# A fused macaron block on one core: GpSimd's long pieces cut in two, the second norm's deviation moved, and the work laid out again

## The chip, the cores and the metric

The kernel runs on one core of one Trainium2 chip. The metric is the device time of one execution in microseconds (us), from the median of several runs. Engines are named as in the profile: PE is TensorE's matmul side, PEld its weight loads, DVE is VectorE, ACT is ScalarE, POOL is GpSimd, SP is SyncE, which only issues DMAs here.

## What is computed

The input is `x` with 2048 tokens of 256 numbers, float32. Three residual steps follow one another:

```python
x = x + 0.5 * ffn(layernorm(x), W_gate, W_qkv)
x = x + attn(layernorm(x), gamma, beta, W_in, b_in, W_out, b_out, W_skip, b_skip)
x = x + 0.5 * ffn(layernorm(x), W_gate, W_qkv)
```

`ffn` is in truth a causal attention with 16 heads of width 16. A softmax over 16 gates picks for every token one head's key and value (the value times the gate), which all 16 query heads share:

```python
idx = argmax(softmax(x @ W_gate.T))
q, k, v = split(x @ W_qkv.T)
k_shared, v_shared = k[idx], gate[idx] * v[idx]
att = softmax(where(causal, q @ k_shared / 4, -inf))      # for each of 16 heads
y = att @ v_shared
```

`attn`, called the branch here, is a gated recurrence: it normalizes its input a second time (so the deviation of the first norm is needed too), computes three gates of width 128 through `W_in`, scans `h = (1 - a) * h + a * b` over the tokens, multiplies with a tanh, projects through `W_out` and adds `x @ W_skip` and two biases.

## The kernel before, in words

**Tiles.** The tokens form four chunks `c` of 512 (4 tiles of 128). `l` is 0 or 1 for the two attention layers and 2 for the branch. `x_sb` holds the whole of x on the chip and is updated in place. An attention unit is (layer, chunk, group of 4 heads), 32 in all; a step is one unit and one tile of 128 keys, 320 steps in all, the first four of each unit on the causal diagonal.

**The work items.** Everything is cut into items, and one list, `ORDER`, says in which order they are issued. Each engine's program is a loop over `ORDER` that takes the items it has a part in, so an engine runs them strictly one behind the other. The items that matter here:

- `("qk", s, k)`: scores of step `s` for a pair of heads, PE line 1670; ACT takes the exponential into `probs` (line 1160, 1024 numbers per partition for a full tile); in a diagonal step POOL then zeroes what lies above the diagonal (the mask, `affine_select`, line 929).
- `("pv", s)`: PE multiplies `probs` with the values (line 1682). It waits for the exponential and, in a diagonal step, for the mask (`s_msk`). `probs` has four buffers.
- `("max", u, n)`: scores with queries on the rows, PE line 1648, so that DVE can take each query's maximum before the exponentials of that unit (`TENSOR_REDUCE`, line 1370, or an add of the mask with a maximum, line 1373); one kind goes through ACT (`relu`, line 1148).
- `("oev", u)`, `("fin", u)`: a unit's sums leave PSUM, are transposed and divided, and POOL adds them to `x_sb` (line 935).
- `prepare(l, c)`: norm, gates, choice of the head, queries and keys of a chunk. `stats` is DVE's mean and variance and then POOL's power to -0.5 (lines 891 and 892), `norm` is ACT's scaling into `u` (line 1042). `halve` is POOL's work for six of the eight chunks: it writes `u` as two float16 parts, a cast and a subtraction over 1024 numbers per partition (lines 941 and 942); `turn` (two, one for each half of the 256 features) are PE's transposes that wait for it. `choose` is DVE's sum over heads (line 1340).
- `branch(c)`: `stats` and `norm` as above, `turn`, `gates` (PE line 1614, then tanh on ACT, then `keep` and `alpha` on POOL, lines 995 and 996, then DVE), `scan` (DVE, then a multiplication on POOL, line 1001), `skip` and `rec` (two each, PE into PSUM; ACT moves `skip` into `sk`, DVE adds `rec` to `x_sb`), `add` (POOL adds `sk` to `x_sb`, 1024 numbers, line 1006).
- `("bias",)`: once, POOL prepares the branch's biases and scales `w_in_sb` (lines 976 to 980).
- `("warm", ...)`: matmuls into banks that nobody reads (lines 1487 and 1490), put where the planner expects PE to be idle.

**Two things POOL does for the branch in the kernel before.** Right behind `stats` of the branch it computes the deviation `s1` for the second norm (lines 895 to 897, needed only by `skip`), and at `norm` it adds the summed biases to the chunk's `x_sb` (line 988, 1024 numbers, needed only by `rec`).

**What sets the order.** `weave()` lays `ORDER` out before the kernel is built. It keeps a clock for each engine and for the PSUM banks, looks a few items ahead and picks what leaves the engines idle least (`LOSS` weighs them); `WEIGHT` says how long each item keeps each engine, `needs` what it depends on, `SIDE_WORK` from which step on the preparations and branches may begin. In the kernel before the masks are no work for POOL in that table: a diagonal `pv` is only held to 850 ns behind its scores instead of 240 (`TO_PE`); `add` and `halve` are entered with POOL times, the deviation, the branch's `norm` and `bias` are not.

## Time and profile before

| what | value |
|---|---|
| median of 3 runs | 934.8 us (933.85 to 934.95) |
| the profiled execution's own time | 931.48 us |
| its span in the trace | 929.6 us |
| mean granted TensorE clock | 0.96 of full |
| PE busy | 860.4 us, 93% of the span |
| DVE busy | 798.4 us, 86% |
| ACT busy | 709.0 us, 76% |
| POOL busy | 212.8 us, 23% |

The profiled execution took 1.9 us more than its span. Two engines are near full, so busy shares alone do not tell what a microsecond on a third one is worth; for that one looks at stretches in which both PE and DVE are idle, and at who ends the idle time. The granted clock is either full or half in any stretch.

### The profile page before, as it was taken

The numbers are of one execution on the slowest core, as the hardware profiler recorded it, in microseconds if no ns is written. First come the engines' busy times: TensorE is split into PE (matmuls) and PEld (weight loads), VectorE is DVE, ScalarE is ACT, GpSimd is POOL, SyncE is SP. The second block draws the span as 40 slices with busy tenths as digits, with TensorE's granted clock in tenths as the row PEclk, the third lists the DMA queues.
The fourth block names the chain that finished last, engine by engine and source line by source line (L and its number), as shares of the span: only waits on it lengthen the run. The fifth ranks groups of instructions, "written<-read, shape, count | busy, mean of one in ns | idle before, by whom it ended". The sixth has DMA issues, their size and how long they took to land.

```text
span 929.6 us, 18195 instructions
## 1 busy us (share of the span) xinstructions
PE 860.4 (93%) x6212; PEld 287.3 (31%) x6212; DVE 798.4 (86%) x2271; ACT 709.0 (76%) x1186; POOL 212.8 (23%) x422
## 2 busy tenths in 40 slices
PE   8897798989899989999999999989799999999997
PEld 6432223222233432223332243333332222222221
DVE  5998898999899789999867999979799999999920
ACT  2264376688879769997789867758689999999997
POOL 2032233111304322032212234144421101110110
PEclk9896689998999999999999999999899999999999
DMA  6110000100010001000010000100020000000000
GB/s 181 47 58 1 1 1 12 48 1 2 1 58 2 1 18 41 2 1 1 2 41 18 2 2 1 59 1 24 1 81 1 2 1 2 24 2 2 1 2 24
DMA packets 20235, 17.97 MB, mean 19 GB/s; under 512 B 4128, under 2 KB 20144, under 8 KB 20144
## 3 DMA queue, kind: packets, MB, share of 16 engines
q1 hardware_dynamic: 19328, 16.00, 5.7%
q8 instruction: 51, 0.84, 0.4%
q10 hardware_dynamic: 816, 0.80, 0.2%
q14 instruction: 40, 0.33, 0.1%
HBM read 10.24 MB, written 6.29 MB: 18 GB/s over the span
## 4 chain that ended last, share of the span: by engine, by line
PE 33%; DVE 13%; issue 7%; ACT 6%; POOL 2%; DMA 0%; POOLq 0%; SPq 0%; DVEq 0%; ACTq 0%
PE ps L1682 13%; PE ps L1648 8%; PE ps L1670 7%; DVE ps L1373 5%; ACT probs L1160 4%; DVE mxp L1370 3%; PE ps L1614 2%; DVE mxp L1373 1%; ACT relu L1148 1%; DVE kv L1340 1%; PE ps L1621 1%; PE ps L1657 1%; PE ps L1566 1%; PE ps L1628 1%; PE ps L1490 1%
## 5 line engine op out<-in xcount | busy, mean ns | idle before, releaser
L1160 ACT ACTIVATE probs<-ps 128x1024 f32<-128x1024 f32 (+5 forms) x841 | 553.9, 735 | 107.3 <-PE ps L1670 102.9
L1370 DVE TENSOR_REDUCE mxp<-ps 128x1 f32<-128x512 f32 x512 | 321.2, 684 | 35.6 <-PE ps L1648 31.3
L1682 PE MATMUL ps<-probs,v_l 128*32 128x512 f32 (+3 forms) x2560 | 306.3, 555 | 19.3 <-POOL probs L929 17.2
L1648 PE MATMUL ps<-k_tl,q_t 48*128 48x512 f16 (+3 forms) x1152 | 253.6, 358 | 12.7 <-DVE mxp L1373 4.6
L1670 PE MATMUL ps<-q_t,k_tl 50*128 50x512 f16 (+3 forms) x1280 | 245.0, 359 | 16.4 <-DMA q_t<-m_row 6.6
L1373 DVE CUSTOM_DVE_ANT_0 ps<-ps,mask 128x384 f32<-128x384 f32 (+3 forms) x512 | 233.6, 525 | 12.5 <-PE ps L1648 11.1
L929 POOL TENSOR_SCALAR_AFFINE_SELECT probs<-probs 128x256 f32<-128x256 f32 x256 | 102.2, 410 | 492.5 <-ACT probs L1160 490.2
L1648 PEld LDWEIGHTS ps<-k_tl,q_t 48*128 48x128 f16 x1152 | 74.1, 95 | 194.7 <-DVE mxp L1370 77.9
L1670 PEld LDWEIGHTS ps<-q_t,k_tl 50*128 50x128 f16 x1280 | 65.0, 94 | 190.5 <-ACT probs L1160 82.7
L1373 DVE DVE_READ_ACCUMULATOR2_ANT mxp<- 128x1 f32 x640 | 90.5, 141 | 0.0
L1373 DVE CUSTOM_DVE_ANT_0 ps<-ps,relu 128x512 f32<-128x512 f32 x128 | 85.8, 717 | 3.2 <-PE ps L1648 2.4
L1682 PEld LDWEIGHTS ps<-probs,v_l 128*32 128x32 f32 x2560 | 53.0, 109 | 107.8 <-issue 82.8
L1148 ACT ACTIVATE relu<-ps 128x512 f32<-128x512 f32 x128 | 71.6, 621 | 4.3 <-PE ps L1648 3.8
L1397 DVE RECIPROCAL rec<-ps 128x16 f32<-128x16 f32 x32 | 8.1, 252 | 39.1 <-PE ps L1657 38.8
L935 POOL TENSOR_TENSOR x_sb<-x_sb,y_att 128x256 f32<-128x256 f32 x32 | 23.3, 727 | 72.5 <-DVE y_att L1401 72.4
L1648 PE MATMUL ps<-kd_tl,q_t 48*128 48x512 f16 x128 | 37.7, 389 | 1.6 <-ACT probs L1160 0.9
L1566 PE MATMUL ps<-wqkv_x,ut_x 128*128 128x512 f16 x144 | 35.1, 380 | 0.5 <-DVE prod L1331 0.3
L1340 DVE TENSOR_REDUCE kv<-prod 128x32 f32<-128x512 f32 x32 | 32.6, 1019 | 0.7
L1168 ACT ACTIVATE o_sb<-ps 128x512 f32<-128x512 f32 x32 | 19.5, 609 | 11.7 <-PE ps L1682 11.7
L1042 ACT ACTIVATE u<-x_sb,shift,rstd 128x256 f32<-128x256 f32 x48 | 25.0, 609 | 2.9 <-POOL shift L892 2.9
L1657 PE MATMUL ps<-ident,o_sb 128*128 128x128 f32 x128 | 22.3, 301 | 2.1 <-DVE mxp L1373 0.7
L1331 DVE TENSOR_TENSOR prod<-ps,pick 128x512 f32<-128x512 f32 x32 | 21.9, 686 | 2.5 <-PE ps L1566 1.7
(167 smaller groups left out, 557.1 us busy)
## 6 DMA issues: line engine op xcount, KB each, us to landing
q_t<-q_scratch SPq DMA_DIRECT2D x96, 64.0 KB, 2.2
q_scratch<-q_part SPq DMA_DIRECT2D x16, 256.0 KB, 2.2
x_sb<-in_L_attn_x_dram SPq DMA_DIRECT2D x4, 512.0 KB, 8.3
out_dram<-x_sb SPq DMA_DIRECT2D x4, 512.0 KB, 3.0
q_t<-m_row SPq DMA_DIRECT2D x64, 4.0 KB
wqkv_n<-in_L_ffn_W_qkv_dram ACTq DMA_DIRECT2D x1, 768.0 KB, 6.9
w_in_sb<-in_L_attn_W_in_dram SPq DMA_DIRECT2D x1, 384.0 KB, 6.0
w_skip_sb<-in_L_attn_W_skip_dram SPq DMA_DIRECT2D x1, 256.0 KB, 5.5
```

Of the source, the lines that this page charges most:

```text
L929: g_.affine_select(out=pr, in_=pr, compare_op=ALU.is_ge, fill=0.0, base=0, pattern=[[0, 2], [1, P]], channel_multiplier=-1).then_inc(s_msk, 1)
L1042: last = a_.activation(u[:, t, :], x_sb[:, TC * c + t, :], ACT.Identity, scale=rstd[:, t:t + 1], bias=shift[:, t:t + 1])
L1148: a_.activation(relu[:, n % RELU_BUFS, :], bank_of(e), ACT.Relu).then_inc(s_ra, 1)
L1160: last = a_.activation(out if len(banks) == 1 else out[:, n:n + 1, :], bank[:, :, P * i:QW], ACT.Exp, scale=SCALE / LIFT ** 2)
L1340: last = v_.tensor_reduce(kv[:, t, :].rearrange("p (a d) -> p a d", a=2), prod[:, :].rearrange("p (a h d) -> p a d h", a=2, h=H), axis=AX, ...
L1370: last = v_.tensor_reduce(to, scores, axis=AX, op=ALU.max)
L1373: last = v_.tensor_tensor_reduce(scores, scores, added, 1.0, LOWEST, ALU.add, ALU.max, accum_out=to)
L1566: last = mm(bank[:, :], ut_x[:, dc, a, t * P:(t + 1) * P], wqkv_x[:, b, dc, D:3 * D], start=n == 0, stop=n == 3 * DC - 1)
L1648: last = mm(bank[:, col:col + w], q_rows(ROWS_X, c, g, hh, i * P, P), keys, start=True, stop=True)
L1657: last = tr(bank[:, i * P:(i + 1) * P], o_sb[:, i * P:(i + 1) * P], ident[:, :])
L1670: last = mm(ps[:, BANK[e][n], P * i:QW], k_cols(ROWS_XM, hh, l, kt, P), q_rows(ROWS_XM, c, g, hh, P * i, QW - P * i), start=True, stop=True)
L1682: last = mm(out_bank[VW * hh:VW * hh + VW, P * i:QW], v_l[:, l, kt, :], probs[:, s % NB, hh, P * i:QW], start=j == 0, stop=j == key_tiles( ...
```

## The change

- `halve` becomes two items, one for each half of the features. Each casts and subtracts 512 numbers per partition, and each `turn` waits only for its own half.
- The branch's `norm` loses its POOL part. It becomes two items `bsum`, 512 numbers each, behind the two `turn`; each `rec` waits for its own.
- The deviation leaves `stats` and becomes an item `dev` behind the first of the `gates`. From the second branch on it waits until ACT has read the former deviation.
- `add` becomes two items of 512 numbers, each behind its own `rec` and `skip`; `stats` of the next layer waits for both.
- The planner: the masks (460), `bias` (3500), `bsum`, `dev`, the first of the `gates` (1250), and the small part of `norm` (1350) now count as POOL time; the rule of 850 ns is gone; `LOSS` is (PE 0.75, DVE 1.0, ACT 1.0) instead of (1.0, 1.0, 0.5), `LOOK` is 400 instead of 300; `SIDE_WORK` has other steps.

```diff
 def branch(c):
-    return [("stats", 2, c), ("norm", 2, c), ("turn", 2, c, 0), ("turn", 2, c, 1), ("gates", c, 0), ("gates", c, 2),
-            ("gates", c, 1), ("scan", c), ("skip", c, 0), ("skip", c, 1), ("rec", c, 0), ("rec", c, 1), ("add", c)]
+    return [("stats", 2, c), ("norm", 2, c), ("turn", 2, c, 0), ("turn", 2, c, 1), ("bsum", c, 0), ("bsum", c, 1),
+            ("gates", c, 0), ("dev", c), ("gates", c, 2), ("gates", c, 1), ("scan", c), ("skip", c, 0), ("skip", c, 1),
+            ("rec", c, 0), ("add", c, 0), ("rec", c, 1), ("add", c, 1)]
...
-             (135, 145, prepare(1, 1)), (164, 172, branch(2)), (172, 174, prepare(1, 2)), (174, 198, branch(3)),
-             (198, 211, prepare(1, 3))]
...
+             (126, 126, branch(1)), (134, 146, prepare(1, 1)), (162, 172, branch(2)), (183, 184, prepare(1, 2)),
+             (204, 204, branch(3)), (226, 226, prepare(1, 3))]
...
-        return 0.44 * width(e[1]), "rows", [("ACT", EXP + EXP_COLUMN * width(e[1]) * 2)]
+        mask = [("POOL", 460)] if STEPS[e[1]][1] < TC else []
+        return 0.44 * width(e[1]), "rows", [("ACT", EXP + EXP_COLUMN * width(e[1]) * 2)] + mask
...
-            t = max(t, ended["qk", e[1], 1] + (850 if j < TC else TO_PE))
+            t = max(t, ended["qk", e[1], 1] + TO_PE)
...
             def stats_of(e):
...
-                if l == 2:
-
-                    own(g_.tensor_tensor(r1[:, :], var1[:, :], half[:, 0:TC], op=ALU.pow))
-                    own(g_.tensor_tensor(r2[:, :], var[:, :], half[:, TC:2 * TC], op=ALU.pow))
-                    g_.tensor_tensor(s1[:, :], r1[:, :], r2[:, :], op=ALU.mult).then_inc(s_dev, 1)
...
             def halve(e):
-                pool.wait_ge(s_ln, NO["norm", e[1], e[2]] + 1)
-                own(g_.tensor_copy(u_x[:, 0, :, :], u[:, :, :]))
-                g_.tensor_tensor(u_x[:, 1, :, :], u[:, :, :], u_x[:, 0, :, :], op=ALU.subtract).then_inc(s_half, 1)
+                _, l, c, dc = e
+                pool.wait_ge(s_ln, NO["norm", l, c] + 1)
+                whole, first = u[:, :, dc * P:(dc + 1) * P], u_x[:, 0, :, dc * P:(dc + 1) * P]
+                own(g_.tensor_copy(first, whole))
+                g_.tensor_tensor(u_x[:, 1, :, dc * P:(dc + 1) * P], whole, first, op=ALU.subtract).then_inc(s_half, 1)
...
+                elif kind == "dev":
+
+                    pool.wait_ge(s_var, NO["stats", 2, e[1]] + 1)
+                    if e[1]:
+
+                        pool.wait_ge(s_ra, FREED["skip", e[1] - 1, 1])
+                    own(g_.tensor_tensor(r1[:, :], var1[:, :], half[:, 0:TC], op=ALU.pow))
...
                 elif kind == "add":
-                    c = e[1]
-                    pool.wait_ge(s_rd, FREED["rec", c, 1])
-                    pool.wait_ge(s_ra, FREED["skip", c, 1])
-                    g_.tensor_tensor(bands(c), bands(c), sk[:, :, :], op=ALU.add).then_inc(s_x2, 1)
+                    _, c, i = e
+                    pool.wait_ge(s_rd, FREED["rec", c, i])
+                    pool.wait_ge(s_ra, FREED["skip", c, i])
+                    rows = bands(c)[:, 2 * i:2 * i + 2, :]
+                    g_.tensor_tensor(rows, rows, sk[:, 2 * i:2 * i + 2, :], op=ALU.add).then_inc(s_x2, 1)
```

The order moves on every engine. Three places show how.

**First place: POOL around the last branch.** In the kernel before the program of POOL reads there:

```order
L891 TENSOR_TENSOR rstd<-var,half 128x4
L892 TENSOR_TENSOR shift<-neg,rstd 128x4
L895 TENSOR_TENSOR r<-var,half 128x4
L896 TENSOR_TENSOR r<-var,half 128x4
L897 TENSOR_TENSOR s<-r 128x4
L935 TENSOR_TENSOR x_sb<-x_sb,y_att 128x4x64
L929 AFFINE_SELECT probs<-probs 128x2x128 x3
L988 TENSOR_TENSOR x_sb<-x_sb,b_out_r 128x1024
L995 TENSOR_SCALAR wqkv_n<-th 128x512
L996 TENSOR_SCALAR alpha<-th 128x512
L1001 TENSOR_TENSOR tc_sb<-hst,tc_sb 128x512
```

and in the changed kernel, where the masks stand on the same line 929, the bias sums on 991, `keep` and `alpha` on 1007 and 1008, and the deviation on 999 to 1001:

```order
L896 TENSOR_TENSOR rstd<-var,half 128x4
L897 TENSOR_TENSOR shift<-neg,rstd 128x4
L929 AFFINE_SELECT probs<-probs 128x2x128 x3
L935 TENSOR_TENSOR x_sb<-x_sb,y_att 128x4x64
L929 AFFINE_SELECT probs<-probs 128x2x128 x2
L991 TENSOR_TENSOR x_sb<-x_sb,b_out_r 128x512 x2
L929 AFFINE_SELECT probs<-probs 128x2x128
L1007 TENSOR_SCALAR wqkv_n<-th 128x512
L1008 TENSOR_SCALAR alpha<-th 128x512
L999 TENSOR_TENSOR r<-var,half 128x4
L1000 TENSOR_TENSOR r<-var,half 128x4
L1001 TENSOR_TENSOR s<-r 128x4
```

The deviation stood ahead of three masks and of the bias sum; now it stands behind `keep` and `alpha`, ahead of one mask, and the masks that stood behind it stand right behind `stats`.

**Second place: POOL at the last `halve`.** Before (the cast on line 941, the subtraction on 942):

```order
L929 AFFINE_SELECT probs<-probs 128x2x128 x5
L935 TENSOR_TENSOR x_sb<-x_sb,y_att 128x4x64
L929 AFFINE_SELECT probs<-probs 128x2x128 x3
L941 CAST u_x<-u 128x1024
L942 TENSOR_TENSOR u_x<-u,u_x 128x1024
L929 AFFINE_SELECT probs<-probs 128x2x128 x5
```

and now (the power and the shift on 896 and 897, the casts on 943, the subtractions on 944):

```order
L929 AFFINE_SELECT probs<-probs 128x2x128 x4
L896 TENSOR_TENSOR rstd<-var,half 128x4
L897 TENSOR_TENSOR shift<-neg,rstd 128x4
L943 CAST u_x<-u 128x4x128
L944 TENSOR_TENSOR u_x<-u,u_x 128x4x128
L943 CAST u_x<-u 128x4x128
L944 TENSOR_TENSOR u_x<-u,u_x 128x4x128
L929 AFFINE_SELECT probs<-probs 128x2x128 x3
```

Eight masks stood close around the one long piece; the four pieces now stand behind `stats` with no mask between, and the whole preparation has moved from steps 199 to 212 to steps 226 to 233. In the same way the last branch has moved from steps 186 to 197 to steps 204 to 209, and now stands nearly in one piece.

**Third place: PE behind the branch's bias (six matmuls with one column).** Before (1670 scores, 1648 scores for maxima, 1682 `pv`, 1657 a `fin`):

```order
L1607 MATMUL ps<-beta_c,w_in_sb 128x1 x6
L1670 MATMUL ps<-q_t,k_tl 128x384 x2
L1657 MATMUL ps<-ident,o_sb 128x128 x4
L1670 MATMUL ps<-q_t,k_tl 128x256 x4
L1682 MATMUL ps<-probs,v_l 32x512 x4
L1648 MATMUL ps<-k_tl,q_t 128x512
L1670 MATMUL ps<-q_t,k_tl 128x128 x4
L1648 MATMUL ps<-k_tl,q_t 128x512
L1682 MATMUL ps<-probs,v_l 32x384 x4
L1670 MATMUL ps<-q_t,k_tl 128x512 x2
L1648 MATMUL ps<-k_tl,q_t 128x512
```

and now (1682 scores, 1660 scores for maxima, 1694 `pv`, 1669 a `fin`, 1502 a warming matmul):

```order
L1619 MATMUL ps<-beta_c,w_in_sb 128x1 x6
L1669 MATMUL ps<-ident,o_sb 128x128 x4
L1682 MATMUL ps<-q_t,k_tl 128x384 x2
L1660 MATMUL ps<-k_tl,q_t 128x512 x2
L1694 MATMUL ps<-probs,v_l 32x512 x4
L1682 MATMUL ps<-q_t,k_tl 128x256 x2
L1660 MATMUL ps<-k_tl,q_t 128x512 x2
L1502 MATMUL ps<-ident,zeros 128x512
L1682 MATMUL ps<-q_t,k_tl 128x256 x2
L1660 MATMUL ps<-k_tl,q_t 128x512 x2
L1502 MATMUL ps<-ident,zeros 128x512
L1682 MATMUL ps<-q_t,k_tl 128x128 x2
```

The `pv` of a diagonal step with 384 columns stood in the ninth of these rows; it now comes in the eighteenth, six below the last one shown, with three warming matmuls ahead of it. In all 92 warming matmuls have become 113.

## Rows read from the trace of the kernel before

**Rows 1.** The profile's page: span, and each engine's busy time.

```profile
span 929.6 us, 18195 instructions
...
PE 860.4 (93%) x6212; PEld 287.3 (31%) x6212; DVE 798.4 (86%) x2271; ACT 709.0 (76%) x1186; POOL 212.8 (23%) x422
```

**Rows 2.** Waits: engine and line, what it waited for, us in total, times, longest.

```profile
POOL probs L929 <- ACT probs L1160: 490.2, 141, 28.7
...
DVE mxp L1370 <- PE ps L1648: 31.3, 40, 3.7
...
PE ps L1682 <- POOL probs L929: 17.2, 10, 3.4
```

**Rows 3.** Timeline of PE: start, us, line, operation, [idle before, releaser].

```profile
141.00 0.85 PE L1682 MATMUL ps<-probs,v_l 128*32 128x384 f32 x8 [3.06 <-POOL probs L929]
...
333.04 0.66 PE L1682 MATMUL ps<-probs,v_l 128*32 128x128 f32 x8 [2.10 <-POOL probs L929]
...
608.59 0.64 PE L1682 MATMUL ps<-probs,v_l 128*32 128x256 f32 x8 [3.39 <-POOL probs L929]
...
662.03 0.66 PE L1682 MATMUL ps<-probs,v_l 128*32 128x128 f32 x8 [2.64 <-POOL probs L929]
```

**Rows 4.** Timeline of POOL, what lay ahead of the masks there.

```profile
136.62 2.49 POOL L980 TENSOR_SCALAR w_in_sb<-w_in_sb,gamma_c 128x384 f32<-128x384 f32 x2
...
605.03 1.01 POOL L895 TENSOR_TENSOR r<-var,half 128x4 f32<-128x4 f32 x1
...
609.13 2.35 POOL L988 TENSOR_TENSOR x_sb<-x_sb,b_out_r 128x1024 f32<-128x1024 f32 x1
...
659.40 2.12 POOL L942 TENSOR_TENSOR u_x<-u,u_x 128x1024 f16<-128x1024 f32 x1
```

**Rows 5.** Windows of 15 us, busy time (count) of each engine, granted clock.

```profile
core 0: us, PE busy (x) PEld busy (x) DVE busy (x) ACT busy (x) POOL busy (x), PEclk, DMA share, GB/s
135.00:150.00 15.00, 11.45 (x84) 3.33 (x84) 10.33 (x26) 9.07 (x22) 10.65 (x15) 0.89 0.01 2
600.00:615.00 15.00, 11.45 (x98) 4.41 (x96) 11.08 (x49) 9.83 (x23) 9.28 (x15) 0.89 0.01 1
...
660.00:675.00 15.00, 12.82 (x107) 6.01 (x107) 10.48 (x35) 7.13 (x14) 4.42 (x8) 0.77 0.00 1
```

**Rows 6.** Windows over stretches at the lower granted clock, same columns.

```profile
73.50:83.70 10.20, 10.20 (x68) 3.94 (x60) 7.35 (x32) 6.87 (x16) 4.08 (x11) 0.50 0.01 2
87.20:100.80 13.60, 12.11 (x65) 3.92 (x65) 10.98 (x40) 5.90 (x11) 4.15 (x9) 0.50 0.01 1
107.60:121.30 13.70, 9.90 (x47) 2.36 (x47) 13.17 (x44) 5.19 (x9) 2.80 (x7) 0.50 0.00 1
141.80:145.20 3.40, 3.40 (x24) 1.00 (x21) 1.65 (x3) 2.77 (x5) 1.19 (x4) 0.50 0.00 0
333.00:336.30 3.30, 3.26 (x27) 1.99 (x27) 0.69 (x1) 1.72 (x3) 0.00 (x0) 0.50 0.00 0
609.40:612.80 3.40, 3.40 (x23) 0.82 (x21) 3.05 (x10) 0.00 (x0) 2.08 (x1) 0.50 0.00 0
660.60:667.40 6.80, 5.33 (x38) 3.09 (x39) 3.15 (x8) 4.22 (x7) 2.82 (x6) 0.50 0.00 0
```

**Rows 7.** Groups by line: engine, tiles, shapes, count, busy us, mean ns, idle.

```profile
L1340 DVE TENSOR_REDUCE kv<-prod 128x32 f32<-128x512 f32 x32 | 32.6, 1019 | 0.7
...
L1331 DVE TENSOR_TENSOR prod<-ps,pick 128x512 f32<-128x512 f32 x32 | 21.9, 686 | 2.5 <-PE ps L1566 1.7 <-PE ps L1581 0.6
...
L1490 PE MATMUL ps<-ident,zeros 128*128 128x512 f16 x46 | 16.9, 392 | 0.0
...
L1006 POOL TENSOR_TENSOR x_sb<-x_sb,wqkv_n 128x1024 f32<-128x1024 f32 x4 | 9.5, 2364 | 2.9 <-DVE x_sb L1431 2.9
...
L1001 POOL TENSOR_TENSOR tc_sb<-hst,tc_sb 128x512 f32<-128x512 f32 x4 | 5.1, 1271 | 22.2 <-DVE hst L1423 22.2
```

**Rows 8.** The masks, line L929: count, duration ns min/median/max, first, last.

```profile
L929 POOL TENSOR_SCALAR_AFFINE_SELECT probs<-probs x256: 399/406/1117, 49.6 to 900.2; 128x256 f32<-128x256 f32 x128
```

More of the change, by code:

```diff
@@ L121, in prepare @@
 def prepare(l, c):
-    return [("stats", l, c), ("norm", l, c)] + ([] if (l, c) in SINGLE else [("halve", l, c)]) + [("turn", l, c, 0), ("turn", l, c, 1), ("gate", l, c), ("pick", l, c),
+    return [("stats", l, c), ("norm", l, c)] + ([] if (l, c) in SINGLE else [("halve", l, c, dc) for dc in range(DC)]) \
+        + [("turn", l, c, 0), ("turn", l, c, 1), ("gate", l, c), ("pick", l, c),
             ("q", l, c, 0), ("kv", l, c, 0), ("choose", l, c, 0), ("qout", l, c, 0), ("q", l, c, 1),
@@ L174 @@
 TO_READER, TO_PE, TO_NEXT = 205, 240, 130
-TURN_MODE, ROW_TRIP, QUERY_TRIP, STATS_TRIP = 110, 2300, 6000, 1500
+TURN_MODE, ROW_TRIP, QUERY_TRIP = 110, 2300, 6000
 FIRST_X, FIRST_W = 6500.0, 8900.0
 EXP, EXP_COLUMN = 65, 0.83
-SAME_MODE, MAXIMA_FIRST, LOOK = 400, 500, 300
-AHEAD, LOSS = 12, (("PE", 1.0), ("DVE", 1.0), ("ACT", 0.5))
+SAME_MODE, MAXIMA_FIRST, LOOK = 400, 500, 400
+AHEAD, LOSS = 12, (("PE", 0.75), ("DVE", 1.0), ("ACT", 1.0))
 WARM_SPARE, WARM_WORK = 200, 217
@@ L209, in weights @@
         return WARM_WORK * e[2], "full", []
+    if e[0] == "gates":
+        return WEIGHT["gates"][0], "full", [[("ACT", 600), ("POOL", 1250)], [("DVE", 600)], [("ACT", 600)]][e[2]]
     pe, then = WEIGHT[e[0]]
@@ L223, in needs @@
         fine = l < 2 and (l, c) not in SINGLE
-        return {"norm": [("stats", l, c)], "halve": [("norm", l, c)], "turn": [("halve" if fine else "norm", l, c)], "pick": [("gate", l, c)],
+        return {"norm": [("stats", l, c)], "halve": [("norm", l, c)],
+                "turn": [("halve", l, c, e[-1]) if fine else ("norm", l, c)], "pick": [("gate", l, c)],
                 "qout": [("q",) + e[1:]], "choose": [("kv",) + e[1:], ("pick", l, c)],
@@ L228, in needs @@
         return [("keys", e[1], 1) if k == "dpack" else ("dpack", e[1])]
+    if k in ("bsum", "dev"):
+        return [("norm", 2, e[1])]
     if k in ("gates", "skip"):
-        return [("turn", 2, e[1], 1)]
+        return [("turn", 2, e[1], 1)] + ([("dev", e[1])] if k == "skip" else [])
     if k in ("scan", "rec"):
-        return [("gates", e[1], 1) if k == "scan" else ("scan", e[1])]
+        return [("gates", e[1], 1)] if k == "scan" else [("scan", e[1]), ("bsum",) + e[1:]]
     if k == "add":
-        return [("rec", e[1], 1), ("skip", e[1], 1)]
+        return [("rec",) + e[1:], ("skip",) + e[1:]]
     if k in ("scale", "split"):
@@ L343, in ready @@
         if e[0] == "stats" and e[1]:
-            before = ("add", e[2]) if e[1] == 1 else ("fin", NG * e[2] + NG - 1)
+            before = ("add", e[2], 1) if e[1] == 1 else ("fin", NG * e[2] + NG - 1)
             return max(t, ended[before] + TO_NEXT) if before in ended else None
@@ L347, in ready @@
             return max(t, ended["qout", e[1], e[2], e[3]] + QUERY_TRIP)
-        back = STATS_TRIP if e[0] == "norm" else TO_PE if weights(e, None)[0] else TO_NEXT
+        back = TO_PE if weights(e, None)[0] else TO_NEXT
         return max([t] + [ended[x] + back for x in needs(e)])
@@ L404, in place @@
             t = at[engine] = max(at[engine], t + reach) + took
+            if e[0] == "qk" and engine == "ACT":
+                for b in self.bank[e]:
+                    self.free[b] = t + TO_PE
             self.done[engine] += took
@@ L413, in place @@
         ended[e] = t
-        if e[0] == "qk":
-            for b in self.bank[e]:
-                self.free[b] = t + TO_PE
         self.said.append(e)
@@ L566 @@
         _last = _e
-HALVES = [_e for _e in ORDER if _e[0] == "halve"]
 def fine(l, c):
@@ L1023, in _ @@
                     scale_root()
-                elif e[0] in ("bias", "scan", "add") or (e[0] == "norm" and e[1] == 2) \
-                        or (e[0] == "gates" and e[2] == 0):
+                elif e[0] in ("bias", "scan", "add", "bsum", "dev") or (e[0] == "gates" and e[2] == 0):
                     recurrence(e)
```

37 lines of the change are left out of this document (20 added, 17 removed).

## The prediction

> **What bounds the kernel now.** I read the profile's page first. PE is busy for 860.4 us of 929.6 and DVE for 798.4 [rows 1], and most of the list is a steady exchange between the two: PE writes scores, DVE takes maxima. POOL has work for 212.8 us [rows 1], so POOL as an engine bounds nothing, and its longest wait is for ACT, 490.2 us in 141 pieces [rows 2]. What costs time on a lightly loaded engine is not its sum but what stands ahead of an urgent piece. So the second view is the list of waits. PE waited for POOL's masks 10 times, 17.2 us in all, and DVE waited for scores from line 1648 for 31.3 us [rows 2]: when PE stands still, DVE runs dry soon after.
>
> The third view is the timeline of PE at these ten places. The four largest waits are 3.06, 2.10, 3.39 and 2.64 us, together 11.2 of the 17.2 us [rows 3]. The fourth is POOL's timeline just before. At 141.00 the scaling of `w_in_sb` had held POOL (2.49 us), at 662.03 the subtraction of a `halve` (2.12), and at 608.59 the deviation, two powers of 1.01 us each of which the first is shown; the bias sum (2.35 us) follows there and pushes the next masks [rows 4]. At 333.04 it was a `halve` again, the same pattern as at 662.03. The smaller six stand behind an `add`, a `halve`, `stats` or a `fin`.
>
> Is PE's idle time there worth time of the kernel? The windows say so: of 15 us DVE was idle for 4.7, 3.9 and 4.5 us in the three stretches that hold the largest waits, and PE for 3.6, 3.6 and 2.2 [rows 5]. Where both are idle, nobody covers for the wait. The clock comes on top: at 141.8, 333, 609.4 and 660.6 PE ran at the lower of its two levels, 0.50 of full (1.2 of 2.4 GHz), for 16.9 us in all, 15.4 of them busy [rows 6], each time within a few microseconds of a wait for a mask. Three longer stretches of the lower level, 37.5 us, lie between 73.5 and 121.3 [rows 6]; no wait for POOL was found in them.
>
> **The change part by part.** The sum is made against the profiled execution, 931.5 us. The median of the three runs, 934.8, stands 3.3 us above it, and that is added at the end.
>
> *(a) Masks no longer stuck.* The deviation leaves the head of the queue, so three masks stand right behind `stats` (the first place of the order). The two halves stand where no mask is urgent (the second place). `bias` still lasts as long, but the planner now knows it and puts the `pv` after it nine rows later (the third place). Of 17.2 us I let 4 stand, since some masks still stand behind a bias sum or between the two `add`: 13.2 us less of PE's idle time. Since DVE was idle in the same windows [rows 5], but not for every microsecond, 10 of these 13.2 count. Bounds: 0, if PE would wait for something else at the same places, and 17.2. **-10**.
>
> *(b) The clock behind those waits.* 15.4 us of busy PE at half level [rows 6] would last 7.7 at full level. Bounds 0 and -7.7; I take half, because branch and preparation thin PE's work there anyway. **-4**.
>
> *(c) Pieces cut in two.* An addition of 1024 numbers took 2.364 us, one of 512 numbers 1.271 [rows 7], so two halves take 2.54, 0.18 us more. There are eight additions cut (four `add`, four bias sums): 1.4 us more for POOL, and some tenths for the six `halve`. All of it lies in POOL's idle time (717 of 929.6 us). If that cover were gone, 1.4 us would be the price. The gain in latency (the first `turn` may begin earlier by half of the subtraction's 2.12 us [rows 4] and half of the cast) hides behind maxima that PE has in store. **0**, bounds -2 and +1.4. The GPSIMD Engine Reference of the Trainium skill (section "Elementwise — side-by-side cycle accounting") gives 4497 ns for an addition of 2048 float32 numbers; an estimate in proportion is 2.25 us for 1024 and 1.12 for 512, which would make cutting free. The rows disagree by the 0.18 us above; by the page the term is 0, by the rows 1.4 us under cover, so the sum stays the same.
>
> *(d) The deviation's new place.* It takes a little over 2 us and is now behind the first of the `gates`, with `skip` on ACT waiting for it. Between them PE has two more gates to compute, so ACT has it in time. Behind it in POOL's queue are one mask and the multiplication for `rec` at the last branch. The wait that this adds is in (f). **0** by itself.
>
> *(e) More warming matmuls.* 113 instead of 92; 46 of them cost 16.9 us of busy PE, 0.37 each [rows 7]. 21 more are 7.7 us if none fell in a gap, nothing if all did. The planner sets them only where it sees a gap: **+1**.
>
> *(f) All other work laid out again.* This is the largest unknown. Two of the four branches, which were spread over 9 and 11 steps, now stand nearly in one piece, and each has a mask behind POOL's wait for the tanh, `keep`, `alpha` and the deviation. I price each at half the longest mask wait, 3.39 [rows 3]: **+3.4**. The bounds come from elsewhere. On the good side the long stretches at the lower clock might go. They hold 32.2 us of busy PE, but DVE was busy for 31.5 of 37.5 us there [rows 6], so DVE takes over after at most 6.0. On the bad side stands DVE work that comes too late: two preparations of the second layer move to later steps, and their products and sums are 4 x (0.686 + 1.019) = 6.8 us each [rows 7], 13.6 for both.
>
> Sum: -10 - 4 + 0 + 0 + 1 + 3.4 = -9.6. The profiled execution would take 921.9 us, the median 934.8 - 9.6 = **925.2 us**.
>
> **The rivals.**
>
> *The early stretches recover too.* The first 121 us are laid out again as well, with warming matmuls between steps 7 and 15, where the kernel before has none. If the clock stays up there and (f) costs nothing, the time is 925.2 - 6.0 - 3.4 = 915.8. For it: the clock was low for 37.5 of the 47.8 us from 73.5 to 121.3. Against it: DVE bounds much of this part (13.17 of 13.70 us in the third stretch [rows 6]), and a few warming matmuls need not hold the clock. Chance 0.20.
>
> *GpSimd's pieces stretch, and nothing is won.* The longest mask took 1.117 us against a median of 0.406 [rows 8]. If the moved pieces (deviation, halves, bias sums) met DVE's work and lasted as much longer, the masks would be late at new places: (a) -3, (b) -1, (e) +1, (f) +3.4, together +0.4, 935.2 us. Against it: 399, 406 as minimum and median of 256 [rows 8] say that stretching is rare. Chance 0.09. The same GPSIMD Engine Reference (section "Key points") speaks for this one: GpSimd shares its SBUF interfaces with VectorE, with contention against DVE instructions that have two SBUF inputs or use a two-port mode. By that rule the time would be this rival's; the rows on the masks bear it out only in their maximum.
>
> *DVE's work comes too late (slower).* The preparation of the last chunk moves from steps 199 to 212 to steps 226 to 233, that of chunk 2 from 173 to 186 to 183 to 192. If DVE runs dry in the short units at steps 192 to 207 and is then behind when the long units begin, idle time earlier is not given back: PE has to wait for maxima instead of for masks. It decides once DVE's idle time between steps 192 and 226 grows by more than one preparation's 6.8 us. One preparation's worth lost is 6.8 us, and with (a) and (b) halved because PE waits for something else in the same places: -5 - 2 + 1 + 3.4 + 6.8 = +4.2, 939.0 us; with both lost 945.8. For it: before, DVE had 10.48 busy of 15 us in the window from 660 [rows 5], close to where work is taken away. Against it: much of that idle time stands behind waits for masks, which go. Chance 0.20.
>
> **How the numbers follow.** The forecast has the other 0.51. The likeliest case gives the time, 925.2. Its own range is 917 to 932: (a) and (b) at their bounds are 10.9 better, and about 7 worse if the half of both stays away. The low end of the whole range is the first rival with what is left of (a) and (b), 915.8 - 3.2 - 3.7 = 909; the high end takes in the slower rival at one preparation, 940. A measurement of this kernel tells 0.2% (1.9 us) from no change. Faster by more: the forecast and the first rival, 0.71; within it: the second rival, 0.09; slower by more: 0.20.
>
> **What would show it.** In the changed kernel's profile the row of PE's line for `pv` waiting for POOL's masks should fall from 17.2 to some 4 us, with none above 2 us. PE's idle time should fall with it, and the stretches at the lower clock behind the waits should be gone, so that the mean granted clock rises from 0.96 to 0.97 or more. ACT should not wait for the deviation at `skip`. POOL's busy time should grow by 1 to 2 us only; growth by 10 would be the stretching rival. DVE waiting for PE's scores by well over 31.3 us, with a low DVE share just before step 226, would be the slower rival. The forecast is wrong if the mask waits fall and the time does not: then they were covered, or something new stands in their place. It is also wrong if the time falls while the mask waits stay, because then the order won it elsewhere.

## The result, and the profile after

The changed kernel takes 930.55 us as the median of 20 runs (925.2 to 932.9), the kernel before 934.89 us (932.8 to 941.0) in the runs beside them. The ratio of the two is 0.994, with a 95% interval of 0.992 to 0.996: 0.6% faster, 4.3 us by the medians. The forecast was 925.2 us in a range of 909 to 940. All ratios here compare runs that nothing disturbed, so they can differ a little from a quotient of two medians.

The profiled execution took 925.4 us, at the fast end of the 20, where the profiled execution of before took 931.5. So the two traces differ by 6.1 us, and 1.8 us of that is the choice of the execution. The page:

```profile
span 923.7 us, 18254 instructions
...
PE 863.7 (94%) x6233; PEld 287.6 (31%) x6233; DVE 799.7 (87%) x2271; ACT 710.0 (77%) x1194; POOL 217.9 (24%) x442
```

Against [rows 1] every engine is busy for a little more, POOL by 5.1 us. PE has been idle for 60.0 us instead of 69.2. The list of waits (engine and line, what it waited for, us in total, times, longest):

```profile
POOL probs L929 <- ACT probs L1172: 480.2, 140, 27.5
...
DVE mxp L1382 <- PE ps L1660: 17.7, 40, 2.9
...
PE ps L1694 <- POOL probs L929: 3.8, 4, 1.9
```

These answer to [rows 2]. PE's waits for masks fell from 17.2 us to 3.8, and DVE waits 17.7 us instead of 31.3 for the scores of its plain maxima. The largest waits that are left, in the timeline of PE, answer to [rows 3]:

```profile
326.71 1.08 PE L1694 MATMUL ps<-probs,v_l 128*32 128x256 f32 x8 [1.94 <-POOL probs L929]
...
642.57 1.07 PE L1694 MATMUL ps<-probs,v_l 128*32 128x512 f32 x8 [0.85 <-POOL probs L929]
```

What lay ahead of the first of them, in POOL's timeline, is something that (a) did not count among what it let stand: the power and the shift behind `stats`, begun when DVE's numbers came, with three masks queued behind. The forecast names `stats` only for small waits.

```profile
324.91 1.02 POOL L896 TENSOR_TENSOR rstd<-var,half 128x4 f32<-128x4 f32 x1 [0.91 <-DVE neg L1237]
326.01 0.20 POOL L897 TENSOR_TENSOR shift<-neg,rstd 128x4 f32<-128x4 f32 x1
326.15 1.14 POOL L929 TENSOR_SCALAR_AFFINE_SELECT probs<-probs 128x256 f32<-128x256 f32 x3
```

In the kernel before, the same power stood between the scaling of `w_in_sb` and the mask of the wait at 141.00 [rows 4], so the scaling was not alone there:

```profile
139.19 1.03 POOL L891 TENSOR_TENSOR rstd<-var,half 128x4 f32<-128x4 f32 x1
```

The windows show where both engines are still short of work (busy time of each engine, count, granted clock, as in [rows 5]):

```profile
core 0: us, PE busy (x) PEld busy (x) DVE busy (x) ACT busy (x) POOL busy (x), PEclk, DMA share, GB/s
90.00:105.00 15.00, 12.03 (x57) 2.95 (x57) 14.88 (x34) 2.90 (x6) 2.81 (x4) 0.74 0.01 2
105.00:120.00 15.00, 10.73 (x57) 2.66 (x56) 13.91 (x46) 6.51 (x13) 3.22 (x8) 0.57 0.00 1
645.00:660.00 15.00, 15.00 (x77) 7.62 (x73) 11.20 (x28) 5.55 (x14) 8.21 (x12) 1.00 0.00 1
```

The long early stretch at half rate is still there: 20.5 us from 97.3 to 117.8, beside a DVE that is busy for 14.88 and 13.91 of 15 us. The stretches behind the mask waits at 141.8, 609.4 and 660.6 [rows 6] are gone; one at 326.0 lasts 6.8 us, where the one at 333 lasted 3.4, one at 203.1 lasts 10.2, and a new one of 6.8 us lies at 397.7. In all the clock was low for 61.4 us before the end of the trace instead of 71.7, and its mean rose from 0.960 to 0.967, as forecast. In the last window PE is full and DVE has 11.20 of 15: that is the last branch, now in one piece.

Warming matmuls into a bank in use are 64 instead of 46, at much the same price [rows 7]:

```profile
L1502 PE MATMUL ps<-ident,zeros 128*128 128x512 f16 x64 | 22.8, 387 | 0.0
```

The cut pieces (count, duration ns min/median/max) answer to [rows 7] and [rows 8]:

```profile
L1019 POOL TENSOR_TENSOR x_sb<-x_sb,wqkv_n x8: 1269/1277/1283, 317.5 to 665.5; 128x512 f32<-128x512 f32 x8
...
L991 POOL TENSOR_TENSOR x_sb<-x_sb,b_out_r x8: 1264/1269/1275, 302.2 to 648.6; 128x512 f32<-128x512 f32 x8
...
L929 POOL TENSOR_SCALAR_AFFINE_SELECT probs<-probs x256: 402/408/1128, 49.9 to 894.2; 128x256 f32<-128x256 f32 x128
```

An addition of 512 numbers takes 1.27 to 1.28 us, as the row of before for that size said. The masks' median is 0.408 us after 0.406: no stretching. POOL's busy time grew by 5.1 us where 1 to 2 were forecast: the cut additions take 1.3 us more, the twelve half `halve` 2.2 us more than the six whole ones, the masks 1.6. ACT does not wait for the deviation: of POOL's results it waits only for the shift, 2.7 us in two waits.

### The profile page after: what moved, and what is told of

Same layout as the page of the kernel before. It is cut to its first block, busy times and chain, and to the rows that moved or that the text cites. A ratio compares the mean times of both kernels' runs of the same rounds, so it can differ in the third digit from the quotient of the medians.

```text
span 923.7 us, 18254 instructions
## 1 busy us (share of the span) xinstructions
PE 863.7 (94%) x6233; PEld 287.6 (31%) x6233; DVE 799.7 (87%) x2271; ACT 710.0 (77%) x1194; POOL 217.9 (24%) x442
## 4 chain that ended last, share of the span: by engine, by line
PE 51%; DVE 30%; issue 8%; ACT 8%; POOL 2%; DMA 1%; SPq 0%; POOLq 0%; DVEq 0%; ACTq 0%
PE ps L1694 18%; PE ps L1660 12%; DVE ps L1385 10%; DVE mxp L1382 10%; PE ps L1682 9%; ACT probs L1172 6%; DVE mxp L1385 2%; PE ps L1626 2%; PE ps L1578 2%; DVE kv L1352 2%; PE ps L1593 1%; PE ps L1633 1%; PE ps L1583 1%; ACT relu L1160 1%; DVE prod L1343 1%
## 5 line engine op out<-in xcount | busy, mean ns | idle before, releaser
L1172 ACT ACTIVATE probs<-ps 128x512 f32<-128x512 f32 (+4 forms) x849 | 554.0, 729 | 100.0 <-PE ps L1682 95.3
L1382 DVE TENSOR_REDUCE mxp<-ps 128x1 f32<-128x512 f32 x512 | 320.1, 682 | 21.2 <-PE ps L1660 17.7
L1660 PE MATMUL ps<-k_tl,q_t 48*128 48x512 f16 (+3 forms) x1152 | 261.1, 356 | 13.4 <-DVE mxp L1385 7.0
L929 POOL TENSOR_SCALAR_AFFINE_SELECT probs<-probs 128x256 f32<-128x256 f32 x256 | 103.8, 417 | 482.2 <-ACT probs L1172 480.2
L896 POOL TENSOR_TENSOR rstd<-var,half 128x4 f32<-128x4 f32 x12 | 13.3, 1105 | 83.4 <-DVE neg L1237 83.0
```

What stands on the lines that cost most here:

```text
L929: g_.affine_select(out=pr, in_=pr, compare_op=ALU.is_ge, fill=0.0, base=0, pattern=[[0, 2], [1, P]], channel_multiplier=-1).then_inc(s_msk, 1)
L1172: last = a_.activation(out if len(banks) == 1 else out[:, n:n + 1, :], bank[:, :, P * i:QW], ACT.Exp, scale=SCALE / LIFT ** 2)
L1382: last = v_.tensor_reduce(to, scores, axis=AX, op=ALU.max)
L1660: last = mm(bank[:, col:col + w], q_rows(ROWS_X, c, g, hh, i * P, P), keys, start=True, stop=True)
```

## The experiments

Times are medians; every ratio is to the kernel before on the same chip in the same session. Its median was 934.4 to 935.4 us in all sessions, so times of different sessions can be compared to about 1 us beside their own spread.

### What do the masks cost in each order?

Both kernels without the masks:

```diff
                 if e[0] == "qk":
-                    _, s, k = e
-                    v, j = STEPS[s]
-                    if j < TC:
-                        pool.wait_ge(s_exp, exp_no(s, k))
-                        pr = probs[:, s % NB, 2 * k:2 * k + 2, P * j:P * j + P]
-                        g_.affine_select(out=pr, in_=pr, compare_op=ALU.is_ge, fill=0.0, base=0,
-                                         pattern=[[0, 2], [1, P]], channel_multiplier=-1).then_inc(s_msk, 1)
+                    return
...
-                    if DIAGONAL[s]:
-                        pe.wait_ge(s_msk, PER_STEP * (DIAGONAL_BEFORE[s] + 1))
```

> The kernel before, with POOL's masks of the diagonal steps left out (all 256) and PE's wait for them, so that the softmax also counts later keys; the order of everything else is the same. Theory (a wait for a mask costs what it lasts, as both PE and DVE stand idle): the 17.2 us of waits go and the time falls by 10 to 17 us, to 918 to 925. Rival (PE finds another wait in the same places, or catches up): the time falls by less than 5 us, to about 930 to 935, though the waits are gone.

Measured: 913.6 us, ratio 0.977 (0.975 to 0.980). That is 21.2 us less than the kernel before, more than the 17.2 us of waits and above the upper end of the expectation. The theory holds and undershot. So a wait for a mask cost at least what it lasted. This run also takes the masks' other effects away, but the last run of this part bears the reading out: it has the old order on the other engines, keeps all masks, has 2.3 us of waits for them, and takes 914.9 us.

> The changed kernel with the 256 masks left out and PE's wait for them; the later keys then count. Theory: only 3.8 us of waits for masks are left to gain, so the time falls by 1 to 4 us from 930.5, to 927 to 929.5. Rival (masks cost through something other than PE's recorded waits, such as the clock or the exponentials' buffers): it falls by more than 5 us.

Measured: 920.2 us, ratio 0.984 (0.981 to 0.987), 9.3 us less than the changed kernel's 0.994 of 935. This is the rival's side: 3.8 us of recorded waits, 9.3 us of cost (6 to 13 by the two intervals). Page, and windows of the stretch from the end of unit 16 to the end of unit 25 (counted from 0), for the old order without masks:

```profile
span 909.1 us, 17842 instructions
...
PE 857.4 (94%) x6212; PEld 289.1 (32%) x6212; DVE 797.9 (88%) x2271; ACT 708.1 (78%) x1186; POOL 113.0 (12%) x166
...
core 0: us, PE busy (x) PEld busy (x) DVE busy (x) ACT busy (x) POOL busy (x), PEclk, DMA share, GB/s
540.00:719.40 179.40, 172.34 (x1334) 63.57 (x1331) 171.54 (x543) 144.96 (x258) 31.29 (x33) 1.00 0.07 22
```

and for the new order without masks, with two windows on its last branch behind:

```profile
span 917.9 us, 17901 instructions
...
PE 862.7 (94%) x6233; PEld 289.4 (32%) x6233; DVE 798.1 (87%) x2271; ACT 709.5 (77%) x1194; POOL 116.0 (13%) x186
...
core 0: us, PE busy (x) PEld busy (x) DVE busy (x) ACT busy (x) POOL busy (x), PEclk, DMA share, GB/s
543.80:727.90 184.10, 175.68 (x1345) 64.21 (x1344) 172.78 (x543) 144.91 (x249) 31.56 (x38) 1.00 0.07 22
...
640.00:650.00 10.00, 10.00 (x49) 4.25 (x48) 6.24 (x14) 4.17 (x10) 5.14 (x7) 1.00 0.01 2
...
650.00:660.00 10.00, 9.78 (x64) 5.59 (x64) 9.52 (x35) 6.77 (x13) 3.93 (x4) 1.00 0.01 2
```

The last branch of the old order lies in these two windows and a few microseconds beyond:

```profile
600.00:610.00 10.00, 10.00 (x47) 5.17 (x47) 8.86 (x41) 3.75 (x6) 2.43 (x3) 1.00 0.01 2
610.00:620.00 10.00, 10.00 (x72) 4.50 (x74) 8.57 (x33) 8.90 (x16) 1.28 (x1) 1.00 0.01 3
```

Here is the main result. Without masks the new order is the slower one, by 0.0068 of 935, 6.4 us (2.5 to 10 by the intervals; no run of the one overlaps a run of the other). The masks cost 21.2 us in the old order and 9.3 in the new, 11.9 less; the order gave 6.4 back; 11.9 - 6.4 = 5.5 us, which is the 0.6% of the result. The split is exact by the way it is made, but the 11.9 and the 6.4 are each good only to about 4 us. In the stretch shown the new order needs 184.1 us instead of 179.4, for 3.3 us more of busy PE (11 of the added matmuls are there), and DVE idles for 11.3 us instead of 7.9. In the window from 640 PE is busy for 10.00 of 10 us and DVE for 6.24: the twelve gate matmuls take 5.4 us in one run there, and from 650 `skip` and `rec` follow, with DVE at 9.52. In the old order the gates stand in one run too (5.3 us from 601.8), with `skip` and `rec` in pieces up to 624, and DVE idles for 2.6 us in its two windows against 4.2 in the two of the new order. So the last branch in one piece accounts for about half of the 3.5 us; where the rest lies was not found.

When the sums of a unit left PSUM (start in us of the eviction into `o_sb`, from the timelines of ACT) shows when the microseconds went. These units have the same work behind them in both orders, within about 3 us by a count of their items:

| unit | before | after | before, no masks | after, no masks |
|---|---|---|---|---|
| 12 | 396.9 | 393.9 | 388.8 | 391.2 |
| 16 | 549.2 | 548.7 | 540.0 | 543.8 |
| 25 | 739.7 | 733.7 | 719.4 | 727.9 |
| 31 | 923.3 | 917.3 | 902.8 | 911.6 |

Without masks the new order is 3.8 us behind at unit 16 and 8.5 at unit 25, then keeps its distance (the profiled executions are 8.8 us apart, the medians 6.6). With masks it is 0.5 us ahead at unit 16 and 6.0 at unit 25, where the old order had two of its four largest waits, at 608.59 and 662.03 [rows 3]. So the gain came in the second layer, and the loss partly there (4.7 us) and partly before it (3.8). Why the masks still cost 9.3 us with 3.8 us of waits is not settled; in the program the mask also lies between exponential and `pv` and so holds `probs` longer, but no run takes that apart.

### The order alone, and the pieces alone

```diff
             def halve(e):
                 _, l, c, dc = e
+                if dc == 0:
+                    return
                 pool.wait_ge(s_ln, NO["norm", l, c] + 1)
-                whole, first = u[:, :, dc * P:(dc + 1) * P], u_x[:, 0, :, dc * P:(dc + 1) * P]
-                own(g_.tensor_copy(first, whole))
-                g_.tensor_tensor(u_x[:, 1, :, dc * P:(dc + 1) * P], whole, first, op=ALU.subtract).then_inc(s_half, 1)
+                own(g_.tensor_copy(u_x[:, 0, :, :], u[:, :, :]))
+                g_.tensor_tensor(u_x[:, 1, :, :], u[:, :, :], u_x[:, 0, :, :], op=ALU.subtract).then_inc(s_half, 2)
```

and `bsum` and `add` in the same way, with the deviation back in `stats_of`.

> The changed kernel's order, list item by list item, but POOL's pieces whole again (a halve, a bias sum and an add each at the place of the second half) and the deviation back right behind the branch's statistics. Theory (the order makes the gain, the pieces lie under cover): 929 to 932, within 2 us of the changed kernel. Rival (the pieces and the deviation's place make it): waits for masks back to 10 us or more and 933 or above.

Measured: 947.1 us, ratio 1.010 (1.007 to 1.014). The theory falls, and so does the forecast's zero for the pieces: on the new order they and the deviation's place are worth 16.5 us by the medians, 15 by the ratios. PE's waits for POOL, and POOL's timeline ahead of the wait at 661.19:

```profile
PE ps L1695 <- POOL probs L935: 9.0, 6, 3.2
...
PE ps L1549 <- POOL u_x L951: 3.9, 3, 1.9
...
658.36 1.02 POOL L901 TENSOR_TENSOR r<-var,half 128x4 f32<-128x4 f32 x1
659.45 1.01 POOL L902 TENSOR_TENSOR r<-var,half 128x4 f32<-128x4 f32 x1
660.54 0.20 POOL L903 TENSOR_TENSOR s<-r 128x4 f32<-128x4 f32 x1
660.69 1.13 POOL L935 TENSOR_SCALAR_AFFINE_SELECT probs<-probs 128x256 f32<-128x256 f32 x3
```

The deviation (658.36 to 660.74) stands ahead of three masks again, and 3.9 us of waiting for `u_x` is new: `turn` stands so close behind `halve` in this order that a whole piece is late. The clock was low for 112.6 us before the end of this trace, against 61.4 in the changed kernel's.

The other way round, the old order with the new pieces:

```diff
-ORDER, BANK = weave()
+_PLAN, BANK = weave()
+ORDER = []
+for _e in _PLAN:
+    if _e[0] == "halve":
+        ORDER += [_e + (0,), _e + (1,)]
+    elif _e[0] == "add":
+        ORDER += [_e + (0,), _e + (1,)]
+    else:
+        ORDER.append(_e)
+        if _e[0] == "norm" and _e[1] == 2:
+            ORDER += [("bsum", _e[2], 0), ("bsum", _e[2], 1)]
+        if _e[0] == "gates" and _e[2] == 0:
+            ORDER.append(("dev", _e[1]))
```

> The order of the kernel before, with every halve, bias sum and add cut in two in the place of the whole one, and the deviation behind the first of the gates. Theory (order makes the gain): 933 to 936, little changed; the wait of 3.39 us behind the deviation goes, the others stay, 17.2 falls to about 12. Rival (pieces make it): 931 or less.

Measured: 932.5 us, ratio 0.997 (0.995 to 0.999): 2.4 us less than the kernel before, between theory and rival. PE's waits for masks, and the one that the deviation had made:

```profile
PE ps L1697 <- POOL probs L932: 14.9, 9, 3.1
...
609.43 0.64 PE L1697 MATMUL ps<-probs,v_l 128*32 128x256 f32 x8 [1.05 <-POOL probs L932]
```

The 3.39 us at 608.59 [rows 3] are 1.05 us; the other large ones stay (3.07, 2.50 and 3.02 us), so the waits fall to 14.9 us and not to 12. In the old order the pieces and the deviation's place gain little, and in the new order they are what it stands on. Neither part explains the result alone.

Which of the two it is, each undone by itself in the new order (the edits are the two halves of the one above):

> The changed kernel with its order and with the deviation at its new place, but each halve, bias sum and add whole, at the place of its second half. The order alone was 16.5 us slower than the changed kernel. Theory (the whole pieces make the first turn, stats and rec late in an order that counts on halves): most of the 16.5 us comes back, 940 to 945. Rival (the deviation's place made it): 930 to 934.

Measured: 936.0 us, ratio 1.001 (0.999 to 1.004), 5.5 us above the changed kernel. PE's waits for masks are 4.2 us, hardly more than the 3.8 there, but its waits for `u_x` are the same as with the order alone:

```profile
PE ps L1550 <- POOL u_x L945: 3.9, 3, 1.9
```

> The changed kernel with its order and its halves, but the deviation right behind the branch's statistics again. Theory (the whole pieces made the loss): 931 to 936, with one or two waits for masks of about 3 us back. Rival (the deviation's place made it): 940 or more.

Measured: 937.6 us, ratio 1.002 (1.000 to 1.005), 7.0 us above it, with two waits of over 3 us back in PE's timeline:

```profile
530.81 1.08 PE L1693 MATMUL ps<-probs,v_l 128*32 128x256 f32 x8 [3.14 <-POOL probs L935]
...
649.18 1.93 PE L1693 MATMUL ps<-probs,v_l 128*32 128x512 f32 x8 [3.19 <-POOL probs L935]
```

Both results lie between theory and rival. By the medians each part costs 5 to 7 us alone and both together 16.5, 4 more than their sum; by the ratios it is 6.8 and 7.8 us alone and 15.2 together. So the two parts count about equally, and that they cost more together than one by one is not shown.

### Is it the planner's knowledge of POOL?

```diff
-SIDE_WORK = [(-3, -3, prepare(0, 1)), (10, 10, [("size",)] + SPLIT), (25, 25, [("bias",)]),
...
+SIDE_WORK = [(-9, -9, prepare(0, 1)), (3, 15, [("size",)] + SPLIT), (25, 25, [("bias",)]), (25, 25, prepare(0, 2)),
...
-SAME_MODE, MAXIMA_FIRST, LOOK = 400, 500, 400
-AHEAD, LOSS = 12, (("PE", 0.75), ("DVE", 1.0), ("ACT", 1.0))
+SAME_MODE, MAXIMA_FIRST, LOOK = 400, 500, 300
+AHEAD, LOSS = 12, (("PE", 1.0), ("DVE", 1.0), ("ACT", 0.5))
```

> The changed kernel's pieces and its POOL times in the planner, but the steps at which preparations and branches may begin, the weights of idle time and the look-ahead as in the kernel before, so that the order differs in between. Theory (knowing POOL's times is what removes the waits for masks): waits for masks at most 6 us and 926 to 932. Rival (the new steps and weights were needed): waits for masks fall too, but 934 or more.

Measured: 955.9 us, ratio 1.021 (1.017 to 1.025). The rival had it right, by far. Page, wait for masks, and a window over the whole span:

```profile
span 953.5 us, 18276 instructions
...
PE 884.3 (93%) x6248; PEld 295.4 (31%) x6248; DVE 799.4 (84%) x2271; ACT 707.2 (74%) x1159; POOL 215.7 (23%) x442
...
PE ps L1694 <- POOL probs L929: 4.4, 3, 2.8
...
0.00:953.50 953.50, 884.29 (x6248) 295.41 (x6248) 799.40 (x2271) 707.19 (x1159) 215.71 (x442) 0.94 0.06 19
```

The waits for masks fell to 4.4 us, as in the changed kernel, and the time rose by 2.1%. PE is busy for 20.6 us more than in the changed kernel, at a mean granted clock below 0.95, and DVE for no more of it, 799.4 us. Whether the steps or the weights were to blame was not tried.

### The warming matmuls

```diff
             def warm(e):
+                if not e[3]:
+                    return
```

> The changed kernel with its order, but without the warming matmuls that stand in the steps (those that go to a bank in use); the ones at the start and at the end stay. Theory (they fill gaps and hold the clock): more time at the lower clock than 61 us and 1 to 8 us slower than 930.5. Rival (they fall where PE would have worked and cost up to 0.37 us each): 2 to 6 us faster than 930.5.

Measured: 935.1 us, ratio 1.001 (0.998 to 1.003), 4.6 us slower than the changed kernel. The page:

```profile
span 929.8 us, 18126 instructions
...
PE 859.8 (92%) x6169; PEld 284.8 (31%) x6169; DVE 799.6 (86%) x2271; ACT 710.8 (76%) x1194; POOL 216.9 (23%) x442
```

PE is busy for 3.9 us less than in the changed kernel, and yet the time is longer: 95.6 us at the lower clock before the end instead of 61.4. The matmuls pay for themselves as a whole.

> The changed kernel without the 256 masks and without the warming matmuls that stand in the steps (the later keys count). With masks left out the changed order took 920.2 us and the old one 913.6. Theory (the 21 added warming matmuls are the 6.6 us between them): without any of them the time is 914 or less. Rival (the layout itself is slower, and the warming matmuls hold the clock as they do with masks): 920 or more.

Measured: 927.2 us, ratio 0.992 (0.990 to 0.995), 7.0 us slower than with them. The theory falls. But the run takes out all 64, of which the kernel before has 46 as well. That the 18 added ones cost nothing, and the layout makes all of the 6.4 us, is likely by this and not shown: it would take a run without the added ones alone.

The forecast's first rival said that the early stretches at half rate hold up to 6 us. To test it, 62 more such matmuls:

```diff
+_planned, ORDER, _more = ORDER, [], 1000
+_spans = [(_planned.index(("oev", 3)), _planned.index(("qk", 22, 0))), (_planned.index(("oev", 7)), _planned.index(("qk", 54, 0)))]
+for _n, _e in enumerate(_planned):
+    if _e[0] == "max" and any(a < _n < b for a, b in _spans):
+        ORDER.append(("warm", _more, 1, True))
+        BANK[ORDER[-1]] = BANK[_e]
+        _more += 1
+    ORDER.append(_e)
```

> The changed kernel with 62 more warming matmuls, one ahead of each bank of maxima in two stretches in which PE ran at half rate beside a full DVE (about 95 to 120 and 203 to 213 us), into the bank that is filled next. Theory (DVE bounds these stretches, so the clock there costs little): within 2 us of 930.5, although the lower clock shrinks by 10 us or more. Rival (the clock there costs as the forecast's first rival had it): 3 to 6 us faster.

Measured: ratio 1.021 (1.018 to 1.024), 25 us slower than the changed kernel by the ratios; single runs took 953.4 to 971.3 us, the median is 964.7. Both theories fall. Window and three rows of PE's timeline (start, us):

```profile
core 0: us, PE busy (x) PEld busy (x) DVE busy (x) ACT busy (x) POOL busy (x), PEclk, DMA share, GB/s
105.00:120.00 15.00, 15.00 (x32) 2.91 (x31) 12.32 (x32) 0.00 (x0) 0.72 (x1) 0.50 0.00 0
...
110.87 0.61 PE L1510 MATMUL ps<-ident 128*128 128x512 f16 x1
111.41 0.61 PE L1671 MATMUL ps<-k_tl,q_t 48*128 48x512 f16 x1
111.95 0.61 PE L1510 MATMUL ps<-ident 128*128 128x512 f16 x1
```

The clock did not rise. PE's records cover the whole window, with a start every 0.54 us, and it stayed at the lower level, from 103.0 on for 34.1 us; in the second stretch it was low for 13.7 us, where it had been for 10.2. In the trace the 62 matmuls take 31.8 us of PE, and PE is busy for 93.4 of the 99.7 us from the end of unit 3 to that of unit 4 and from unit 7 to unit 8, which take 70.5 us in the changed kernel; DVE is busy for 68.5 us there. PE had become the bound. So what the clock costs in these stretches was not measured by this run and stays open.

### POOL's program out of step with the others

If the old order lost to masks only, the masks can be freed without laying the other engines out again. POOL runs its own list:

```diff
+MOVES = [(("bias",), ("kpack", 0, 2)), (("stats", 0, 3), ("qk", 63, 1)), (("halve", 1, 0, 1), ("qk", 87, 1)),
+         (("add", 1, 0), ("qk", 131, 1)), (("add", 1, 1), ("add", 1, 0)), (("halve", 1, 2, 1), ("qk", 177, 1)),
+         (("stats", 2, 3), ("qk", 187, 1)), (("add", 3, 0), ("qk", 197, 1)), (("add", 3, 1), ("add", 3, 0)),
+         (("stats", 1, 3), ("qk", 199, 1)), (("halve", 1, 3, 0), ("qk", 203, 1)), (("halve", 1, 3, 1), ("qk", 204, 1))]
+POOL_ORDER = list(ORDER)
+for _e, _after in MOVES:
+    assert POOL_ORDER.index(_e) < POOL_ORDER.index(_after), (_e, _after)
+    POOL_ORDER.remove(_e)
+    POOL_ORDER.insert(POOL_ORDER.index(_after) + 1, _e)
...
-            for e in ORDER:
+            for e in POOL_ORDER:
```

> The order of the kernel before on PE, DVE, ACT and SP, with the cut pieces and the deviation behind the first of the gates; on POOL alone twelve items are moved behind masks that PE needs sooner (the bias work by ten steps, two statistics, four halves, the adds of two branches, the last branch's statistics). Theory (the old order is the better one and lost its time to mask waits only): waits for masks fall from 14.9 us to 5 or less, and the time to 920 to 926, below both kernels. Rival (the new order itself carried the gain, or the moved pieces make turns and statistics late): 929 or more.

Measured: 922.3 us, ratio 0.987 (0.985 to 0.989), below both kernels and in the range of the theory.

```profile
PE ps L1709 <- POOL probs L944: 7.0, 7, 2.5
...
176.99 0.43 PE L1709 MATMUL ps<-probs,v_l 128*32 128x128 f32 x8 [2.54 <-POOL probs L944]
```

7.0 us of waits are left, the largest one of our own making: the bias work had been put just ahead of the last mask of step 35. So once more, with that move changed and one added:

```diff
-MOVES = [(("bias",), ("kpack", 0, 2)), (("stats", 0, 3), ("qk", 63, 1)), (("halve", 1, 0, 1), ("qk", 87, 1)),
+MOVES = [(("bias",), ("qk", 56, 1)), (("stats", 0, 2), ("qk", 27, 0)), (("stats", 0, 3), ("qk", 63, 1)), (("halve", 1, 0, 1), ("qk", 87, 1)),
```

> As the run with POOL's own order (922.3 us), but the bias work comes behind the masks of step 56 instead of in a diagonal stretch, and the statistics of chunk 2 behind the first mask of step 27. Those two held masks for 2.54 and 1.33 us. Theory: waits for masks fall from 7.0 to about 3.5 us and the time by 2 to 5 us more, to 917 to 920.5. Rival (the statistics come late instead, or DVE covers these waits): 921.5 to 924.

Measured: **914.9 us**, ratio 0.977 (0.975 to 0.980): 19.5 us below the kernel before and 15.7 below the changed one, and better than expected.

```profile
span 913.5 us, 18223 instructions
...
PE 855.9 (94%) x6212; PEld 286.5 (31%) x6212; DVE 798.3 (87%) x2271; ACT 708.2 (78%) x1186; POOL 216.7 (24%) x442
...
DVE mxp L1397 <- PE ps L1675: 18.2, 34, 2.8
...
PE ps L1709 <- POOL probs L944: 2.3, 4, 1.2
```

It reaches the time of the old order without any masks (913.6 us). The pieces alone had brought the old order to 932.5 us; the other 17.6 us are thirteen items moved on an engine that is busy for a quarter of the time: the bias work past 29 masks, the others past four at most.

## Why the prediction was right in sign and too large

- **What bounds the kernel.** Right. The waits for masks fell as said, from 17.2 to 3.8 us (4 forecast). That both PE and DVE stand idle behind them was right too, and stronger than said.
- **(a) and (b), -14.** Measured together as the difference of what the masks cost in the two orders: 21.2 - 9.3 = 11.9 us, good to about 4. Close, but not in the way of the working. The forecast took 14 us for 13.2 us of waits, 1.06 for each. In the old order all waits together cost 21.2 us for 17.2, 1.23 for each; and in the new one 9.3 us of cost stayed where the forecast had some 4 us of waits and their share of it. What part of this is the clock, (b), no run separates. The stretches at the lower clock behind the old waits went, except near 326 to 333, and others came.
- **(c), 0.** The sizes of the additions were right, 1.27 us for 512 numbers; the `halve` grew by 2.2 us and not by some tenths. The GPSIMD Engine Reference of the Trainium skill (section "Elementwise — side-by-side cycle accounting") led to an estimate of 1.12 us by proportion, and the measurement decides against that. The zero was about right for the old order only (with (d): -2.4). In the new order, whole pieces cost 5.5 us. The step that failed is that the gain in latency "hides behind maxima that PE has in store": with whole pieces in the new order PE waits for `u_x` for 3.9 us in three waits, so there is too little in store between `halve` and `turn`.
- **(d), 0 by itself.** Wrong in the new order as well: undone it costs 7.0 us, with two waits of over 3 us.
- **(e), +1.** The matmuls in the steps gain 4.6 us as a whole; what the added ones do by themselves (18 of the 21 are among these) was not run.
- **(f), +3.4.** The term that was mis-sized, with (e): 4.4 forecast, 6.4 measured without masks. The place was right in part: around the last branch, now in one piece, DVE idles for about 1.7 us more, and 3.8 us were lost before the second layer. Its price was taken from a mask wait, which had nothing to do with it, so that it came out near is luck.
- **The sum.** -9.6 forecast, -5.5 by the ratio (11.9 won, 6.4 lost), -4.3 by the medians. 2.1 us of the gap is (a) and (b), 2.0 is (e) and (f); both are within what these measurements can tell. The forecast's own range is not what its sum gives either: 10.9 us better than 925.2 is 914.3 and not 917.
- **The rivals.** Stretched pieces: no, the masks' median is 0.408 us. The Trainium skill's GPSIMD Engine Reference (section "Key points") speaks of contention for SBUF interfaces with VectorE; no run here shows it, in (a) or elsewhere. The early stretches did not recover. DVE's late work: without masks it did idle 3.5 us more between units 16 and 25, half of the 6.8 us that this rival put on one preparation, but half of that lies at the last branch. With masks it idled for less there than before, 11.9 us instead of 18.5, and its waits for scores fell to 17.7 us.

## What to carry to other kernels

Where one list orders all engines, a lightly loaded engine can need its own priorities more than the list needs its times. Here moving 13 items on POOL alone gained 17.6 us on top of the cut pieces, while pieces and a new layout of everything gained 4.3. To price a wait, take away what causes it and time that, in both layouts; here this split a small net gain into some 12 us won and some 6 us lost, which no wait list showed. Do not read a part's worth off the layout it was not made for: the same pieces, with the deviation's place, were worth 2.4 us in one order and 15 or more in the other.
